# Attention kernel on one core: PE rounds of two steps, scores in four PSUM banks, stacked heads for the out-projection, one 1024-column exponential

## The chip, the cores and the metric

The kernel runs on one core of a Trainium2 chip. The metric is device microseconds of one execution, taken as the median of several runs. The engines are named as in the profile: PE is TensorE (PEld its weight loads), DVE VectorE, ACT ScalarE, POOL GpSimd, SP the engine that here issues nearly all the DMAs. Each engine works through its own queue in order, and they meet at semaphores.

## The reference

Input `x` is 4 x 1024 x 128 in f32. One pre-norm transformer layer is computed:

```
x = x + attention(layernorm(x))         # 16 heads of 64, rotary on the first 32, no mask
x = x + ffn(layernorm(x))               # low rank: x U1 V1 -> gelu -> U2 V2 (rank 32, width 512)

q, k, v = heads(x Wq), heads(x Wk), heads(x Wv);  q, k = rope(q), rope(k)
attn = softmax(q k^T / 8);  out = concat(attn v) Wout + bout
```

Attention is nearly all of it: 64 pairs of batch and head, each with a 1024 x 1024 score matrix.

## The kernel before

Heads are taken in groups of `GH` = 4 (16 iterations: 4 batches x 4 groups). A head has `KT` = 8 blocks of 128 keys, so an iteration has `STEPS` = 32 steps, and there are 512 steps in all. Iteration 0 and iteration 15 are written out, iterations 1 to 14 are a hardware loop.

A step `t` of head `h` and key block `kt` does this:

- **Scores** (`pe_scores`, L386 and L387): keys on the partitions, all 1024 queries as columns, in two halves of 512. Q and K are split into a high and a low f16 part and stacked, so a half takes two accumulating full-array matmuls. The result is `S`, 128 x 1024 f32, two PSUM banks, one copy.
- **Exponential** (`act_step`, L516): ScalarE takes each half of `S` and writes `PF`, which has `SLOTS` = 8 slots of 128 x 1024 f32.
- **Values** (`pe_values`, L398): `PF` of the step `PV_LAG` = 2 back, times V (128 x 64, f32), added up over the head in one PSUM bank `O`: columns tiled in two, one half of the queries in each 64 partitions. `O` has two copies, heads alternate.
- **Unit** (`pe_unit`, L407, and `dve_max`, L603): for the row maximum of the head that comes `LEAD` = 12 steps later, an eighth of the queries (128) against all keys into `M`, 128 x 1024, two banks, one copy: two matmuls on 64 rows each, side by side in the array. VectorE takes the maximum over the 1024 columns. The next unit waits for this (`max_read`). The eight maxima go through ScalarE and a DMA into a row of Q's stack, where they are subtracted inside the score matmul.
- **Sums for the denominators** (`pool_sum`, L676, `dve_sum`, L610 and L613): GpSimd adds two slots of `PF` at each even step, VectorE adds those pairs to `SUM`.
- **Tiles** (`pe_tiles`): at chosen steps PE also does a tile of other work into one of two banks `T`: projections of Q, K and V for the next group (L310, L316), the denominators of two heads (`den_tile`, L326: a matmul with ones), and the out-projection (`out_tiles`, L338: two tiles at one step, 64-row matmuls for the two query halves side by side in the array, summed over two heads). Which step has which tile stands in `QK_AT`, `V_AT`, `DEN_AT` and `OUT_AT`. The tile is then read by ScalarE (`act_tiles`, at the front of ScalarE's step) and by VectorE (`dve_tiles`, one step later): rotary product and shuffle L530 and L532, low part L535, add to X L539. GpSimd finishes the rotation (`rot_add` L652 and L655, `rot_low` L663). PE waits before tile n for the readers of tile n - 2 (`before`, `freed`).

PE's order inside a step is values, tiles, scores, unit (`pe_step`). VectorE's is tile readers, sums, the inverse of the denominators (L619), the norm of two heads' output (`dve_norm`, L625), the maximum. The order of SP's queue is written out in `HAND_ORDER`: the new Q and K are handed from `STAGE` to `QK` by four DMAs a head (`hand_over`, L708 and L709), which can start only when GpSimd's last low part is done (`rot_lo`) and the head's scores have been read, and which the unit of step 20 waits for (`handed`). `max` is the row of maxima, `sums`, `inverse` and `spread` are the denominators' way out to be inverted and back, spread over 64 partitions, into `RB`; `wo` is a load of the output weights for two heads.

Ahead of the loop stand the first projections and 12 units; behind it the last denominators, the out-projection and the feed-forward part.

Of the kernel before, what the change touches and what calls it, by code (L numbers as in the profile page):

```python
# [15 lines left out]
P = 128  # L16
# [12 lines left out]
PV_LAG = 2  # L29
# [20 lines left out]
APPLY_AT = (17, 18, 19, 20, 25, 26)  # L50
BIAS_AT = (19, 21, 23, 24, 27, 28)
TURN_X0_AT = (23, 24, 25, 26, 29, 30)
TURN_X_AT = (4, 6, 9, 11, 14, 16)
DOWN_AT = (7, 12, 13, 15, 18, 19)

HAND_ORDER = [("qk", 3), ("wo", 0), ("max", 1), ("sums", 1), ("inverse", 1), ("spread", 1), ("max", 2), ("qk", 0),
              ("qk", 1), ("wo", 1), ("sums", 0), ("max", 3), ("inverse", 0), ("spread", 0), ("qk", 2), ("max", 4)]


def tiles_of(first, last):  # L60

    out = []
    for t in range(STEPS):
# [12 lines left out]
        if t in OUT_AT and not (first and OUT_AT[t]):  # L76
            out += [(t, "out", (OUT_AT[t], z)) for z in range(2)]
# [6 lines left out]
assert PRE_TILES % 2 == 0 and MID_TILES % 2 == 0  # L84


class Iteration:


    def __init__(self, i, first=False, last=False):  # L90
        self.i, self.first, self.last = i, first, last
        self.tiles = tiles_of(first, last)
        self.tile0 = PRE_TILES if first else PRE_TILES + FIRST_TILES + (i - 1) * MID_TILES
        self.turn = 0 if first else FIRST_TILES % 2
# [11 lines left out]

    def bank(self, n):
        return (n + self.turn) % 2


def build(nc, x_d, wq_d, wkv_d, wout_d, bout_d, u1_d, v1_d, b1_d, u2_d, v2_d, b2_d, rope_d, ident_d, out_d):
    with ExitStack() as ctx:
# [15 lines left out]
        WO = sb("WO", [P, 2, 2, D], F32)  # L128
# [54 lines left out]
        HB = [half[:, z * 512:(z + 1) * 512] for half in (S, M) for z in range(2)]  # L183


        x_in = [sem(f"x_in{b}") for b in range(B)]
        w_in, small_in, rope_in = sem("w_in"), sem("small_in"), sem("rope_in")
        wo_in = [sem(f"wo_in{p}") for p in range(2)]
# [47 lines left out]
        def before(it, n):  # L236

            if n >= 2:
                return it.tiles[n - 2][1:], it
            if it.first:  # L240
                return ("proj", PROJ[-2 + n]), Iteration(-1)
            prev = Iteration(it.i - 1) if not (isinstance(it.i, int) and it.i == 1) else Iteration(0, first=True)
            return prev.tiles[n - 2][1:], prev
# [55 lines left out]
        def proj_tile(e, args, g, bank):  # L299
# [5 lines left out]
            if w == "v":  # L305
                cols = bass.ds((gi * GH + 2 * c) * DH, 2 * DH)
                for r in range(4):
                    rows = bass.ds(b * N + (4 * t + r) * P, P)
                    for n, (xp, wp) in enumerate(((0, 0), (0, 1), (1, 0))):
                        mm = e.matmul(T[bank][:, r * P:(r + 1) * P], XT[:, xp, rows], WV[:, wp, cols],  # L310
# [810 lines left out]
```

## Time and profile before

| | |
|---|---|
| median of 3 runs | 1562.38 us (1561.53 to 1564.28) |
| profiled execution | 1561.73 us, of it the span of the instructions 1559.8 us |
| mean granted PE clock | 0.988 of 2.4 GHz |
| busy: PE, DVE, POOL, ACT | 1481, 1170, 969, 753 us |
| instructions | 26676 |

The busy time of an engine is the time in which at least one of its instructions runs. Matmuls are pipelined and their ends modelled, so what a matmul costs PE is read from the start of one group to the start of the next, not from its duration. A line of the timeline merges equal instructions that follow each other and gives their count as x4; what stands in brackets is the idle time in front, and who ended it.

### The profile page before, as it was taken

To read this page: it belongs to the slowest core of one execution; us is meant where nothing else is said; L and a number is where in the kernel's file an instruction comes from. 1 tells how busy PE (TensorE), PEld (TensorE's weight loads), DVE (VectorE), ACT (ScalarE), POOL (GpSimd) and SP (SyncE) were. 2 spreads that over 40 slices of the span, in tenths; PEclk is the share of its full clock that TensorE was granted. 3 is DMA by queue.
4 is the path that set the end of the run, shared out by engine and by line. 5 is a ranking of instruction groups with operands and counts; after the bars stand their busy time and mean duration, and the time that the engine had idled before them with its cause. 6 is when DMAs were issued, how large, how long until landed. Compare 5 with 4: busy or idle time off the path is not lost.

```text
span 1559.8 us, 26676 instructions
## 1 busy us (share of the span) xinstructions
PE 1481.2 (95%) x7801; PEld 504.4 (32%) x7801; DVE 1169.7 (75%) x1297; ACT 752.9 (48%) x1448; POOL 969.3 (62%) x501
## 2 busy tenths in 40 slices
PE   3799999999999999999999999999999999999887
PEld 1233333333333333333333333333333333333324
DVE  7778777778777777877777777777777787777834
ACT  2254545444454544545454454545444454544464
POOL 4498857657384756748475664847566584757831
PEclk9799999999999999999999999999999999999998
DMA  4322031222203122220313122131312212131002
GB/s 145 75 45 58 15 79 26 61 52 57 58 14 78 36 62 41 57 58 14 78 37 69 32 58 57 24 68 37 78 24 58 57 34 61 34 78 24 19 17 66
DMA packets 78386, 79.69 MB, mean 51 GB/s; under 512 B 28212, under 2 KB 45112, under 8 KB 78104
## 3 DMA queue, kind: packets, MB, share of 16 engines
q1 hardware_dynamic: 76912, 78.36, 22.1%
q10 hardware_dynamic: 1448, 1.00, 0.2%
q8 instruction: 14, 0.23, 0.1%
q14 instruction: 12, 0.10, 0.0%
HBM read 26.23 MB, written 2.36 MB: 18 GB/s over the span
## 4 chain that ended last, share of the span: by engine, by line
PE 73%; DVE 10%; POOL 8%; issue 7%; ACT 1%; DMA 1%; SPq 0%; DVEq 0%; POOLq 0%; ACTq 0%
PE O L398 25%; PE S L386 12%; PE S L387 11%; PE M L407 10%; PE TILE L316 5%; DVE MX L603 5%; POOL SA L676 4%; PE TILE L338 4%; PE TILE L310 3%; PE TILE L326 2%; DVE SUM L613 1%; DVE OS L625 1%; POOL STAGE L663 1%; POOL QK L812 1%; POOL RSTD L277 1%
## 5 line engine op out<-in xcount | busy, mean ns | idle before, releaser
L676 POOL TENSOR_TENSOR SA<-PF 128x1024 f32<-128x1024 f32 x256 | 632.4, 2475 | 378.3 <-DVE SUM L610 194.6
L603 DVE TENSOR_REDUCE MX<-M 128x1 f32<-128x1024 f32 x506 | 617.1, 1220 | 314.5 <-PE M L407 312.5
L516 ACT ACTIVATE PF<-S 128x512 f32<-128x512 f32 x1024 | 555.5, 595 | 479.8 <-PE S L387 479.8
L398 PE MATMUL O<-PF,V 128*64 128x512 f32 x2048 | 552.1, 618 | 0.0
L386 PE MATMUL S<-QK 128*128 128x512 f16 x1024 | 392.4, 383 | 1.6 <-DVE MX L603 1.6
L387 PE MATMUL S<-QK 128*128 128x512 f16 x1024 | 389.1, 380 | 0.0
L407 PE MATMUL M<-QK 64*128 64x512 f16 x1012 | 222.8, 437 | 29.8 <-DVE MX L603 23.2
L613 DVE TENSOR_TENSOR SUM<-SUM,SA 128x1024 f32<-128x1024 f32 x128 | 199.0, 1555 | 7.9 <-POOL SA L676 7.9
L386 PEld LDWEIGHTS S<-QK 128*128 128x128 f16 x1024 | 99.7, 97 | 309.7 <-ACT PF L516 188.3
L652 POOL TENSOR_TENSOR T<-T,ROPE 128x512 f32<-128x512 f32 x60 | 76.5, 1274 | 139.3 <-DVE T L532 139.3
L407 PEld LDWEIGHTS M<-QK 64*128 64x128 f16 x1012 | 72.5, 139 | 247.7 <-issue 204.3
L398 PEld LDWEIGHTS O<-PF,V 128*64 128x64 f32 x2048 | 101.3, 134 | 118.9 <-ACT PF L516 79.1
L387 PEld LDWEIGHTS S<-QK 128*128 128x128 f16 x1024 | 100.6, 98 | 75.9 <-issue 0.8
L316 PE MATMUL TILE<-XT,WQK 128*128 (+1 forms) x384 | 108.6, 394 | 5.5 <-DVE XT L1019 2.5
L655 POOL TENSOR_TENSOR YR<-T 128x512 f32<-128x512 f32 x60 | 101.4, 1690 | 4.7
L663 POOL TENSOR_TENSOR STAGE<-YR,STAGE 128x512 f16<-128x512 f32 x64 | 88.3, 1380 | 17.3 <-ACT STAGE L454 17.3
L610 DVE TENSOR_TENSOR SUM<-SA 128x1024 f32<-128x1024 f32 x64 | 79.6, 1243 | 18.0 <-POOL SA L676 18.0
L436 ACT ACTIVATE STAGE<-TILE 128x512 f16<-128x512 f32 x64 | 38.2, 597 | 94.2 <-PE TILE L316 94.2
L444 ACT ACTIVATE V<-TILE 128x512 f32<-128x512 f32 x64 | 38.2, 597 | 89.2 <-PE TILE L310 89.2
L625 DVE TENSOR_TENSOR OS<-OS,RB 128x1024 f32<-128x1024 f32 x32 | 71.3, 2229 | 9.6 <-DMA RB<-den 9.6
L338 PE MATMUL TILE<-WO,OS 64*128 64x128 f32 x1024 | 67.5, 283 | 8.9 <-DVE OS L625 5.9
L338 PEld LDWEIGHTS TILE<-WO,OS 64*128 64x128 f32 x1024 | 61.3, 192 | 34.4 <-issue 33.6
(75 smaller groups left out, 732.6 us busy)
## 6 DMA issues: line engine op xcount, KB each, us to landing
QK<-STAGE SPq DMA_DIRECT2D x128, 256.0 KB, 3.9
QK<-STAGE SPq DMA_DIRECT2D x128, 128.0 KB, 3.1
RB<-den SPq DMA_DIRECT2D x128, 128.0 KB, 2.9
WO<-in_L_attn_Wout SPq DMA_DIRECT2D x64, 64.0 KB, 2.8
X<-in_L_attn_queries SPq DMA_DIRECT2D x4, 512.0 KB, 12.7
RT<-DS SPq DMA_DIRECT2D x128, 2.0 KB, 1.7
out<-X SPq DMA_DIRECT2D x8, 256.0 KB, 2.4
WRAW<-in_L_attn_Wkv SPq DMA_DIRECT2D x1, 1024.0 KB, 8.6
```

The costliest lines, as they stand in the source:

```text
L316: mm = e.matmul(T[bank][:, :], WQK[:, "qk".index(w), wp, kind, cols], XT[:, xp, rows], start=(n == 0), stop=(n == 2))
L338: mm = e.matmul(T[banks[z]][:, j * P:(j + 1) * P], OS[rows, parity, hh, j * P:(j + 1) * P], WO[rows, parity, hh, :], start=(hh == 0), stop ...
L386: e.matmul(S[:, rows], KHL[:, h, keys], QHH[:, h, rows], start=True, stop=False)
L387: e.matmul(S[:, rows], KMH[:, h, keys], QML[:, h, rows], start=False, stop=True).then_inc(scored, 1)
L398: mm = e.matmul(O[h % 2][DH * z:DH * z + DH, :], V[:, h, kt * DH:(kt + 1) * DH], PF[:, t % SLOTS, z * HALF:(z + 1) * HALF], start=(kt == 0 ...
L407: mm = e.matmul(bank[:, keys], QHH[rows, place, q:N:KT], (KHL, KMH)[c][rows, place, keys], start=True, stop=True)
L516: e.activation(PF[:, t % SLOTS, z * HALF:(z + 1) * HALF], S[:, z * HALF:(z + 1) * HALF], ACT.Exp, scale=EXP_SCALE).then_inc(exped, 1)
L603: e.tensor_reduce(MX[:, place % 2, q:q + 1], bank[:, :], AX, ALU.max).then_inc(max_read, 1)
L613: e.tensor_tensor(SUM[:, h % 2, :], SUM[:, h % 2, :], SA[:, part - 1, :], ALU.add).then_inc(summed, 1)
L655: e.tensor_tensor(YR[:, :], T1[:, :], T2[:, :], ALU.add).then_inc(rot_sum, 1)
L663: e.tensor_tensor(LOW[w][:, 0, cols], YR[:, :], HIGH[w][:, 0, cols], ALU.subtract).then_inc(rot_lo, 1)
L676: e.tensor_tensor(SA[:, (t // 2) % 2, :], PF[:, t % SLOTS, :], PF[:, t % SLOTS + 1, :], ALU.add).then_inc(two_summed, 1)
```

## The change

- PE works in rounds of two steps (`pe_step`): at an even step the values of two steps (4 and 3 back; `PV_LAG` is 4), the unit, the scores, the tiles; at an odd step the scores, the tiles, the unit.
- `S` has two copies (four banks), used by even and odd steps. For these banks `O` has one copy and `T` has one; PE waits before a tile for the readers of the one just before it. In the prologue and the tail, halves of `M` stand in as second banks.
- ScalarE's step has one exponential over 1024 columns, and its tile readers stand behind the exponential instead of in front. `exped` counts steps and not halves.
- The out-projection: two heads are stacked on the 128 partitions of `OS` (ScalarE copies `O` out in two pieces of 64 partitions), so each tile is four 128-row matmuls per 512 queries, and the two tiles (query halves) stand at steps of their own. All of `Wout` lies in SBUF, loaded once at the start; `weights_over` and its DMAs are gone.
- The steps of nearly all tiles, inverses, sums and statistics are moved, as the tables show. VectorE's inverse stands before the sum in a step. SP's spread does not wait for the norm any more.
- The 12 leading units go round three pairs of banks instead of two.

```diff
-PV_LAG = 2
+PV_LAG = 4
-QK_AT = (1, 3, 4, 6, 7, 9, 11, 12)
-V_AT = {8: (1, 0), 10: (1, 1), 21: (0, 0), 22: (0, 1)}
-DEN_AT = {5: 1, 20: 0}
+QK_AT = (1, 3, 5, 7, 9, 11, 13, 15)
+V_AT = {8: (1, 0), 10: (1, 1), 22: (0, 0), 24: (0, 1)}
+DEN_AT = {6: 1, 20: 0}
 INVERT_AT = {9: 1, 23: 0}
 NORM_AT = {16: 1, 26: 0}
-OUT_AT = {17: 1, 28: 0}
-SUM_AT = {6: 0, 1: 1, 3: 2}
-STATS_AT = {6: 2, 22: 3}
+OUT_AT = {17: (1, 0), 19: (1, 1), 28: (0, 0), 30: (0, 1)}
+SUM_AT = {7: 0, 1: 1, 3: 2}
+STATS_AT = {6: 2, 14: 3}
...
-        S = pb("S", [P, N], F32)
+        S = pb("S", [P, 2, N], F32)
         M = pb("M", [P, N], F32)
-        O = [pb(f"O{n}", [P, HALF], F32) for n in range(2)]
-        T = [pb(f"TILE{n}", [P, 512], F32) for n in range(2)]
+        O = pb("O", [P, HALF], F32)
+        T = pb("TILE", [P, 512], F32)
...
-            if n >= 2:
-                return it.tiles[n - 2][1:], it
+            if n >= 1:
+                return it.tiles[n - 1][1:], it
...
-        def out_tiles(e, q, parity, i, banks):
-            e.wait_ge(wo_in[parity], 32 * (i + 1))
+        def out_tile(e, q, parity, pair, z, bank):
             e.wait_ge(normed, q + 1)
             for j in range(4):
-                for hh in range(2):
-                    for z in range(2):
-                        rows = slice(DH * z, DH * z + DH)
-                        mm = e.matmul(T[banks[z]][:, j * P:(j + 1) * P], OS[rows, parity, hh, j * P:(j + 1) * P],
-                                      WO[rows, parity, hh, :], start=(hh == 0), stop=(hh == 1))
+                mm = e.matmul(bank[:, j * P:(j + 1) * P], OS[:, parity, z, j * P:(j + 1) * P], WO[:, pair, :],
+                              start=True, stop=True)
...
-                wait(e, exped, 2 * n + z - 1)
+                wait(e, exped, n - 1)
...
         def pe_step(e, it, t):
-            for back in (t - PV_LAG,):
-                if back >= 0:
-                    pe_values(e, it.step(back), it.i * GH + back // KT, back, it.i)
-                elif not it.first:
-                    pe_values(e, it.step(back), it.i * GH - 1, back + STEPS, it.i - 1)
-            pe_tiles(e, it, t)
-            pe_scores(e, it, t)
-            u = t + LEAD
-            if not (it.last and u >= STEPS):
-                ...
-                pe_unit(e, it.step(u), place, q, M)
+            u = t + LEAD
+            if t % 2 == 0:
+                for back in (t - PV_LAG, t - PV_LAG + 1):
+                    if back >= 0:
+                        pe_values(e, it.step(back), it.i * GH + back // KT, back, it.i)
+                    elif not it.first:
+                        pe_values(e, it.step(back), it.i * GH - 1, back + STEPS, it.i - 1)
+                if not (it.last and u >= STEPS):
+                    pe_next_unit(e, it, u)
+            pe_scores(e, it, t)
+            pe_tiles(e, it, t)
+            if t % 2 == 1 and not (it.last and u >= STEPS):
+                pe_next_unit(e, it, u)
...
-            for z in range(2):
-                e.wait_ge(scored, 2 * n + z + 1)
-                ...
-                e.activation(PF[:, t % SLOTS, z * HALF:(z + 1) * HALF], S[:, z * HALF:(z + 1) * HALF], ACT.Exp,
-                             scale=EXP_SCALE).then_inc(exped, 1)
+            e.wait_ge(scored, 2 * n + 2)
+            ...
+            e.activation(PF[:, t % SLOTS, :], S[:, t % 2, :], ACT.Exp, scale=EXP_SCALE).then_inc(exped, 1)
+            act_tiles(e, it, t)
...
-            e.activation(OS[:, h // 2, h % 2, :], O[h % 2][:, :], ACT.Copy).then_inc(o_copied, 1)
+            for z in range(2):
+                cp = e.activation(OS[rows, h // 2, z, :], O[DH * z:DH * z + DH, :], ACT.Copy)
+            cp.then_inc(o_copied, 1)
...
-                wait(sp, normed, q)
-        def weights_over(sp, it, p):
-        ...
+            sp.dma_start(WO[:, :, :], wout_d.rearrange("(c p) n -> p c n", p=P)).then_inc(wo_in, 16)
```

## Rows read from the trace of the kernel before

**Rows 1.** The page, part 1: busy time of each engine.

```profile
PE 1481.2 (95%) x7801; PEld 504.4 (32%) x7801; DVE 1169.7 (75%) x1297; ACT 752.9 (48%) x1448; POOL 969.3 (62%) x501
```

**Rows 2.** Busy time of each engine in one middle iteration of 32 steps.

```profile
677.28:767.62 90.34, 89.12 (x475) 29.88 (x473) 69.13 (x69) 44.45 (x87) 56.67 (x29) 1.00 0.22 50
```

**Rows 3.** PE's timeline over a step without tile: start, duration, line, tile.

```profile
729.91 1.08 PE L398 MATMUL O<-PF,V 128*64 128x512 f32 x4
730.92 0.39 PE L386 MATMUL S<-QK 128*128 128x512 f16 x1
731.15 0.38 PE L387 MATMUL S<-QK 128*128 128x512 f16 x1
...
731.58 0.38 PE L387 MATMUL S<-QK 128*128 128x512 f16 x1
731.89 0.44 PE L407 MATMUL M<-QK 64*128 64x512 f16 x2
732.26 1.08 PE L398 MATMUL O<-PF,V 128*64 128x512 f32 x4
```

**Rows 4.** The same timeline, a unit that waits.

```profile
737.08 0.44 PE L407 MATMUL M<-QK 64*128 64x512 f16 x2 [0.42 <-DVE MX L603]
```

**Rows 5.** PE's timeline behind the last step, two value groups together.

```profile
1506.64 0.38 PE L387 MATMUL S<-QK 128*128 128x512 f16 x1
1506.94 1.94 PE L398 MATMUL O<-PF,V 128*64 128x512 f32 x8
1508.82 0.60 PE L954 MATMUL S<-STAGE,V1P 96*128 96x512 f16 x2
```

**Rows 6.** PE's timeline near the start of the first iteration.

```profile
58.03 0.65 PE L407 MATMUL M<-QK 64*128 64x512 f16 x2
58.61 1.46 PE L316 MATMUL TILE<-XT,WQK 128*128 128x512 f16 x3
```

**Rows 7.** PE's timeline: an out-projection, and full-array f32 tiles in the tail.

```profile
740.81 2.06 PE L338 MATMUL TILE<-WO,OS 64*128 64x128 f32 x32
...
1547.29 1.06 PE L980 MATMUL TILE<-V,QK 128*128 128x128 f32 x8
```

**Rows 8.** ScalarE's timeline, the exponentials of the step of rows 3.

```profile
731.57 1.09 ACT L516 ACTIVATE PF<-S 128x512 f32<-128x512 f32 x2 [1.09 <-PE S L387]
```

**Rows 9.** VectorE's timeline, two maxima.

```profile
732.38 1.22 DVE L603 TENSOR_REDUCE MX<-M 128x1 f32<-128x1024 f32 x1 [0.44 <-PE M L407]
...
735.81 1.22 DVE L603 TENSOR_REDUCE MX<-M 128x1 f32<-128x1024 f32 x1
```

**Rows 10.** Groups by line, VectorE: count, busy us, mean ns, idle before.

```profile
L613 DVE TENSOR_TENSOR SUM<-SUM,SA 128x1024 f32<-128x1024 f32 x128 | 199.0, 1555 | 7.9 <-POOL SA L676 7.9
L625 DVE TENSOR_TENSOR OS<-OS,RB 128x1024 f32<-128x1024 f32 x32 | 71.3, 2229 | 9.6 <-DMA RB<-den 9.6
L532 DVE STREAM_SHUFFLE T<-TILE 128x512 f32<-128x512 f32 x64 | 46.7, 730 | 0.0
L530 DVE TENSOR_TENSOR T<-TILE,ROPE 128x512 f32<-128x512 f32 x64 | 43.5, 680 | 0.4 <-PE TILE L316 0.4
```

**Rows 11.** GpSimd by line and in the timeline, a hand-over's issue and landing.

```profile
L676 POOL TENSOR_TENSOR SA<-PF 128x1024 f32<-128x1024 f32 x256 | 632.4, 2475 | 378.3 <-DVE SUM L610 194.6 <-ACT PF L516 132.2 <-DVE SUM L613 51.5
L652 POOL TENSOR_TENSOR T<-T,ROPE 128x512 f32<-128x512 f32 x60 | 76.5, 1274 | 139.3 <-DVE T L532 139.3
L655 POOL TENSOR_TENSOR YR<-T 128x512 f32<-128x512 f32 x60 | 101.4, 1690 | 4.7
...
725.74 2.14 POOL L663 TENSOR_TENSOR STAGE<-YR,STAGE 128x512 f16<-128x512 f32 x1
738.27 1.16 POOL L663 TENSOR_TENSOR STAGE<-YR,STAGE 128x512 f16<-128x512 f32 x1
...
741.62 0.68 SPq L709 DMA_DIRECT2D QK<-STAGE  x1
DMA to landing us min/median/max: 3.0/3.9/4.6
```

More of the change, by code:

```diff
@@ L75, in tiles_of @@
             out.append((t, "den", DEN_AT[t]))
-        if t in OUT_AT and not (first and OUT_AT[t]):
-            out += [(t, "out", (OUT_AT[t], z)) for z in range(2)]
+        if t in OUT_AT and not (first and OUT_AT[t][0]):
+            out.append((t, "out", OUT_AT[t]))
     return out
@@ L309, in proj_tile @@
                     for n, (xp, wp) in enumerate(((0, 0), (0, 1), (1, 0))):
-                        mm = e.matmul(T[bank][:, r * P:(r + 1) * P], XT[:, xp, rows], WV[:, wp, cols],
+                        mm = e.matmul(bank[:, r * P:(r + 1) * P], XT[:, xp, rows], WV[:, wp, cols],
                                       start=(n == 0), stop=(n == 2))
@@ L315, in proj_tile @@
                 for n, (xp, wp) in enumerate(((0, 0), (0, 1), (1, 0))):
-                    mm = e.matmul(T[bank][:, :], WQK[:, "qk".index(w), wp, kind, cols], XT[:, xp, rows],
+                    mm = e.matmul(bank, WQK[:, "qk".index(w), wp, kind, cols], XT[:, xp, rows],
                                   start=(n == 0), stop=(n == 2))
@@ L602, in dve_max @@
                 wait(e, max_found, head - 1)
-            e.tensor_reduce(MX[:, place % 2, q:q + 1], bank[:, :], AX, ALU.max).then_inc(max_read, 1)
+            e.tensor_reduce(MX[:, place % 2, q:q + 1], bank, AX, ALU.max).then_inc(max_read, 1)
         def dve_sum(e, head, h, part):
@@ L632, in dve_step @@
                 dve_last(e, t)
-            h, kt = t // KT, t % KT
+            if t in INVERT_AT and not (it.first and INVERT_AT[t]):
+                dve_invert(e, it.pair(INVERT_AT[t]))
             if kt in SUM_AT and SUM_AT[kt] == 0:
@@ L637, in dve_step @@
                 dve_sum(e, it.i * GH + h - 1, (h - 1) % GH, SUM_AT[kt])
-            if t in INVERT_AT and not (it.first and INVERT_AT[t]):
-                dve_invert(e, it.pair(INVERT_AT[t]))
             if t in NORM_AT and not (it.first and NORM_AT[t]):
                 dve_norm(e, it.pair(NORM_AT[t]), NORM_AT[t])
-            u = t + LEAD
             if not (it.last and u >= STEPS):
-                dve_max(e, it.step(u), it.i * GH + u // KT, (u // KT) % GH, u % KT, M)
+                dve_max(e, it.step(u), it.i * GH + u // KT, (u // KT) % GH, u % KT, M[:, :])
         def rot_add(e, args, g):
@@ L672, in pool_sum @@
         def pool_sum(e, t, pair, free):
-            e.wait_ge(exped, 4 * pair + 4)
+            e.wait_ge(exped, 2 * pair + 2)
             wait(e, summed, free)
@@ L729, in den_over @@
                 sp.wait_ge(inverse_turned, 16 * (q + 1))
[L730 removed]
                 for s in range(4):
                     hh, z = s // 2, s % 2
[L733 removed]
+                    sp.dma_start(RB[DH * hh:DH * hh + DH, z, :],
                                  den_d[s:s + 1, :].broadcast_to([DH, HALF])).then_inc(spread_in, 16)
[L736 to L742 removed]
         def sp_iteration(sp, it):
@@ L778, in build @@
         tail0 = lastit.tile0 + len(lastit.tiles)
-        den_bank = lastit.bank(len(lastit.tiles))
         @block.sync
@@ L942, in body @@
                 for t in range(STEPS):
+                    if it.first and OUT_AT.get(t) == (0, 0):
+                        e.wait_ge(wo_in, 16)
                     pe_step(e, it, t)
@@ L998, in _ @@
                 if c == 1:
-                    kind, args = lastit.tiles[-1][1:]
-                    pe.wait_ge(*freed(kind, args, lastit))
                     pe.wait_ge(den_copied, PAIRS)
-                    out_tiles(pe, PAIRS - 1, 1, GROUPS - 1, (1 - den_bank, den_bank))
+                    for z in range(2):
+                        out_tile(pe, PAIRS - 1, 1, HEADS // 2 - 1, z, TB[z])
                 if c == 3:
                     for late in range(EARLY, FC):
-                        down_tile(pe, late, late % 2)
+                        down_tile(pe, late, TB[late % 2])
                 if c >= 1:
```

161 lines of the change are left out of this document (75 added, 86 removed).

## The prediction

> **What bounds the kernel now.** I read the page's first part, then the busy time of whole loop iterations, then TensorE's timeline inside one of them, and last VectorE's rows. PE is busy for 95% of the span, VectorE for 75%, GpSimd 62%, ScalarE 48% [rows 1]. A middle iteration of 32 steps takes 90.34 us with PE busy for 89.12 [rows 2]; sixteen of these are 1445 of the 1559.8 us of the span. The feed-forward part begins behind the last step at 1508.82 [rows 5]. In the timeline PE runs without a hole: a step without a projection tile goes from one value group (729.91) to the next (732.26), so 2.35 us [rows 3]. The reader is to see the seams in it: the values take 1.01 us to the first score, scores 0.97 to the unit M, the unit 0.37 to the next values. Scores are full-array, units are two row tiles of 64, values two column tiles of 64. Two scores further PE is 0.43 us further (731.15 to 731.58), so one is 0.215 and four with a seam make 0.97: the seam from scores to M is 0.11 us; the unit's 512 columns would be 0.21 too, so its seam is 0.16. The kernel is thus bound by the order of PE's queue, not by ScalarE: S being free late shows only as early weight loads that wait under a running value group. Real PE holes are few: M waits for the previous maximum, as at 737.08 with 0.42 us [rows 4], and about as much once more near the other out-projection: 1.2 us an iteration, the 90.34 less the 89.12 of busy time.
>
> **The change, part by part.**
>
> *The order of PE's queue.* Two steps now cost 4.70 us. In the new order a pair is: values of two steps, M, scores, scores, M (tiles stand behind each score block). Two value groups together are shown behind the last step: eight matmuls start at 1506.94 and the next operation at 1508.82, 1.88 us, where two separate groups take 2.02 [rows 5]. Two score blocks that touch take 0.97 + 4 x 0.215 = 1.83 us, where two separate ones take 1.94. M to values stays 0.37. Values to M is not in the trace; I take it like values to scores, with no change, and bound it by a gain or a loss of 0.05 (the span of the seams seen). M straight to full-array work stands only at the start, at the lower clock: M at 58.03, tile at 58.61, 0.58 us [rows 6], of which 0.43 are columns at 1.2 GHz, so a seam of 0.15. At 2.4 GHz it lies between the 0.10 of scores to M and the 0.16 of M to values; I take 0.13, so 0.34 us. The pair: 1.88 + 0.34 + 1.83 + 0.37 = 4.42, which saves 0.28 us. 512 steps are 256 pairs: 72 us, with bounds of 51 and 92 (0.08 either way for both seams together).
>
> The Trainium skill says in TensorEngine Tiling (Array Packing), Key Properties, that changing the tiling mode drains TensorE, while changing only the tile does not. The rows agree as to where the seams are: at each of the three changes of [rows 3]. By that rule alone, at one equal price of 0.16 for each change, six changes a pair become four, and 256 pairs would give back 82 us; the rows price them unequally, so my 72 stands.
>
> *Tiles.* The projections are the same instructions, now beside scores of the same form: no change. The denominator tile stood between values and scores and stands now between two score blocks; it gets one more seam of 0.09 (scores to values, 1506.64 to 1506.94, less 0.215) [rows 5]: 32 x 0.09 = 3 us lost. The out-projection had 32 half-row matmul records in 2.06 us for both tiles; it becomes two tiles of 8 full records. The same form (128 rows, 128 columns, f32) stands in the tail, 8 records in 1.06 us [rows 7]. So stacking heads halves the count and gains nothing: 2 x 1.06 against 2.06, some 2 us lost over 32 pairs; bounded by 5 us either way, as its seams to the scores vanish. Together -5 us.
>
> *One exponential of 1024 columns.* Two of 512 take 1.08 us with their overlap [rows 8]; one of 1024 has the same columns, so between 1.0 and 1.1, and I take 1.04. ScalarE is not on the path, S has two copies, and values come four steps late, so all this is worth nothing by itself. What hides it is two steps of PE work (4.4 us). The copies out are two of 64 partitions and not one of 128, 0.6 us more per head, with the same cover.
>
> *One tile bank in place of two.* Each tile on PE now waits until the previous one has been read, and ScalarE reads it behind the exponential. It matters where tiles stand in an even and the next odd step and ScalarE reads the first: steps 8 and 9, 10 and 11 (V, then a projection), and 6 and 7. Before, the first half's exponential at 731.57 starts 0.42 after that half's second score at 731.15 [rows 3, 8]. The one of step 8 then starts 3 x 0.215 + 0.42 = 1.07 us after that step's first score, ends after 1.04, the copy of V (512 columns) takes 0.60, and PE gets the bank at 2.75. PE is there at 0.86 + 0.65 + 0.86 = 2.37, a little later with the seams of V's twelve matmuls. So a hole of 0.35 us twice, none behind the denominators: 0.7 us an iteration. Everywhere else 0.37 + 1.88 + 0.34 + 0.86 = 3.45 us lie between two tiles, more than the 3.0 in which VectorE is through with a maximum, a product and a shuffle.
>
> *M against VectorE.* M has one copy. The maximum starts 0.49 after M (731.89, then 732.38), lasts 1.23 [rows 9], and a waiting M starts 0.05 after it (735.81 + 1.23, then 737.08); the next VectorE instruction can start after 1.15. So M to M is never under 1.77. The new PE spacings are 0.34 + 1.83 = 2.17 plus tiles from the even M to the odd, and 0.37 + 1.88 = 2.25 from the odd to the next even: both longer, without VectorE's other work. I carried that work through 32 steps, each maximum starting at the later of "its M + 0.49" and "the previous maximum + 1.15 + the other work", with the mean durations: sums 1.55 (steps 1, 3 and, at the most, 7 of each head), product and shuffle 1.4 at steps 2, 6, 10, 14, norm 2.2 at 16 and 26 [rows 10]. VectorE works some 69 us of 88, so it catches up mostly. It is late at two places: at 16 the norm puts M of 17 off by 0.2 and with the sum of 17 that of 18 by 0.45; at 26 the norm puts 27 off by 0.65 and 28 by 0.45. That is 1.75 us an iteration, against 1.2 before.
>
> The Trainium skill (GPSIMD Engine Reference, Specifications) says that GpSimd shares SBUF interfaces with VectorE and contends with its instructions of two SBUF inputs. The sum's mean of 1.55 us against 1.23 for the maximum, which reads one input over the same columns, agrees. By that rule shorter iterations overlap these more; that way is rival B below, whose price comes from rows.
>
> *Hand-over of Q and K.* The last rotated tile moves from step 11 to 13, so GpSimd's last low part moves from step 15 to 17, while M of step 20 still needs the first head's hand-over. In the trace, low part ended at 739.43, its fourth transfer was issued at 741.62 and lands 3.9 later: 6.1 us [rows 11]. By the spacings above, product and shuffle of step 14 end 40.1 us into the new iteration; GpSimd then does 3.0 of rotation and two sums of 2.48 until 48.0, and the low part of 1.2 until 49.2; handed over at 55.3. M of 20 is due at 56. The cover is under 1 us; I put 0.3 us an iteration on it. SP's queue in front is shorter (two weight transfers and the wait on the norm left it). The denominators' way has 2.5 to 3 steps to the inverse; if that is 1 us short, VectorE waits and not PE, inside its slack of 19 us.
>
> *The rest.* Output weights are loaded once in the prologue (512 KB behind X, needed at step 28): nothing. The 12 leading units use three banks, but VectorE's 1.15 a maximum sets their pace: nothing. In the tail four value groups stand there and not two, the other two left the loop. The first iteration has VectorE's statistics at steps 6 and 14 beside a product and shuffle; I take 2 us more stall for it and 2 for the last.
>
> *Sum.* New holes an iteration 0.7 + 1.75 + 0.3 = 2.75, old 1.2, so 1.55 x 15 = 23 us, and 4 for the ends: 27. -72 + 5 + 27 = -40 us. The profiled execution took 1561.7 us (span 1559.8); minus 40 is 1521.7, and the median of the runs is 0.7 above it: 1522 us.
>
> **Rivals.**
> A: the holes do not come (tile reads are sooner, VectorE's late moments fall into slack). For it: 20 us an iteration of VectorE are free. Against: the norm's 2.2 us plus two maxima and a sum (6.1) are longer than a pair (4.4). Time: 1562 - 72 + 5 + 4 = 1499.
> B: VectorE becomes the bound in stretches. A low part of GpSimd takes 2.14 us at one place and 1.16 at another [rows 11]; if VectorE's eight sums of steps 1 and 3 and its two norms were each 1 us longer in the same way, a pair, which leaves 4.42 - 2.3 - 1.55 = 0.57 us beside two maxima and a sum, would hide 0.57 of each. Of the other 0.43, 4.3 us an iteration, I estimate that a third finds no tile to hide behind: 1.4 x 15 = 22 us. Time: 1544. Against: GpSimd's work is the same, and the means hold both kinds.
> C: slower. The hand-over becomes the end of the chain. Step 20's M waits at the head of PE's queue, with scores, tiles and all values behind it, and VectorE and ScalarE soon wait for these. If each of the five GpSimd instructions in front is 1 us longer (as 2.14 is than 1.16) [rows 11], it is handed over at 60.3: a hole of 4.3 us, 4.0 beyond the forecast, in each of 15 iterations, 60 us: 1582. It makes the kernel slower once the hole passes 2.7 us (40 / 15) beyond what I have in. Against: the low part at just this place took 1.16.
> D: the change does not do what it says, because a seam is paid at each group of matmuls whatever stands next. Then the 72 us go and so do most holes, for PE is as slow as before: 1562. Against: the 1.88 us of [rows 5].
>
> **How the numbers follow.** The forecast 0.52, A 0.14, B 0.17, C 0.12, D 0.05. The time is the forecast's, 1522. The range reaches to A's 1499 and past B towards no change, which takes in most of the seams' bounds: 1499 to 1558. Of this kernel 0.2%, 3 us, is what can be told from no change. Faster: forecast, A, B, less a little: 0.81. Same 0.06, slower 0.13.
>
> **What would show it.** Right: PE's timeline has eight value matmuls in 1.88 us, M to scores 0.34, a plain pair of 4.4 us, and an iteration of 87.7 us; waits of M for the maximum near steps 17, 18, 27, 28; a tile at steps 9 and 11 that waits for ScalarE's copy of V by 0.35 us; next to no wait of M for the hand-over. Wrong: plain pairs of 4.6 us or more (the seams), more than 4 us of holes per iteration (VectorE or tile bank), or a wait of M for the hand-over of over 1 us in each iteration.

## The result, and the profile after

The changed kernel takes 1568.10 us (median; 1566.81 to 1569.64) against 1562.38 (1561.19 to 1564.28): a ratio of 1.0034, 95% interval 1.0022 to 1.0046, so a little slower. The forecast was 1522 us and a range that ended at 1558; both were wrong. Rows of before are named by their groups in the section of rows.

The page of the changed kernel, part 1 and the first line of part 4, against [rows 1], and below it the first line of part 4 of the kernel before:

```profile
PE 1429.6 (91%) x7289; PEld 548.1 (35%) x7289; DVE 1225.1 (78%) x1297; ACT 746.3 (48%) x1000; POOL 972.5 (62%) x501
...
PE 38%; issue 18%; POOL 17%; DVE 15%; DMA 5%; ACT 4%; SPq 2%; DVEq 0%; POOLq 0%; ACTq 0%
```

```profile
PE 73%; DVE 10%; POOL 8%; issue 7%; ACT 1%; DMA 1%; SPq 0%; DVEq 0%; POOLq 0%; ACTq 0%
```

PE is busy for 51.6 us less, as meant, and the span is still 5.2 us longer (1565.0). VectorE does the same 1297 instructions in 55 us more. In the chain that ended last, PE had 73% before and has 38% now; the rest went mostly to issue, POOL and VectorE.

Busy time of each engine in a middle iteration of the changed kernel, against [rows 2] (window, length, PE, PEld, DVE, ACT, POOL, clock):

```profile
682.47:772.70 90.23, 85.67 (x442) 32.63 (x441) 72.90 (x69) 43.93 (x58) 56.82 (x28) 1.00 0.21 47
```

An iteration is as long as before (90.34) with 3.45 us less PE work in it. The clock is full in both. So the loop lost nothing and gained nothing: what the seams gave was spent on holes. PE's timeline in this iteration shows both (start, duration; in brackets the idle time in front and what ended it):

```profile
700.99 0.44 PE L397 MATMUL M<-QK 64*128 64x512 f16 x2 [0.66 <-DVE MX L600]
...
737.65 0.44 PE L397 MATMUL M<-QK 64*128 64x512 f16 x2
738.02 1.94 PE L388 MATMUL O<-PF,V 128*64 128x512 f32 x8
739.89 0.44 PE L397 MATMUL M<-QK 64*128 64x512 f16 x2
740.26 0.39 PE L376 MATMUL S<-QK 128*128 128x512 f16 x1
...
742.78 1.15 PE L330 MATMUL TILE<-WO,OS 128*128 x8 [0.62 <-DVE OS L622]
...
746.95 0.43 PE L397 MATMUL M<-QK 64*128 64x512 f16 x2 [0.78 <-DVE MX L600]
747.32 0.39 PE L376 MATMUL S<-QK 128*128 128x512 f16 x1
...
750.04 0.44 PE L397 MATMUL M<-QK 64*128 64x512 f16 x2
...
752.86 0.44 PE L397 MATMUL M<-QK 64*128 64x512 f16 x2 [0.52 <-DMA QK<-STAGE]
...
766.77 1.94 PE L388 MATMUL O<-PF,V 128*64 128x512 f32 x8
768.64 0.44 PE L397 MATMUL M<-QK 64*128 64x512 f16 x2
...
770.53 0.38 PE L377 MATMUL S<-QK 128*128 128x512 f16 x1
772.33 0.44 PE L397 MATMUL M<-QK 64*128 64x512 f16 x2 [1.42 <-DVE MX L600]
772.70 1.51 PE L388 MATMUL O<-PF,V 128*64 128x512 f32 x6
```

M to values takes 0.37 (737.65 to 738.02), eight value matmuls 1.87 and M to scores 0.37 (739.89 to 740.26, where 0.34 was forecast): the seams are nearly there as forecast. The pair from 766.77 to 772.70 takes 5.93, of which the last M's wait is 1.49 (by the distance to the score in front of it), so 4.44 without it. Earlier in the same iteration, the two tiles of steps 9 and 11 wait for ScalarE:

```profile
718.62 0.83 PE L306 MATMUL TILE<-WV,XT 128*128 x12
720.56 0.82 PE L312 MATMUL TILE<-XT,WQK 128*128 x3 [0.24 <-ACT V L441]
```

By distances between starts, the holes of one iteration are: 0.73 where M of step 2 waits for a maximum (at 700.99), 0.42 and 0.41 at the tiles of steps 9 and 11, 0.9 at the out-projection of 17 (it waits for the norm), 0.85 at M of 18, 0.58 at M of 20 (the hand-over), 1.49 at M of 27; with 0.15 at M of step 0 that is 5.5 us. The kernel before has 1.35 by the same count (0.86 and 0.49). The busy times make it 4.6 and 1.2 only, since the modelled ends of the records in front reach a little into each hole.

The groups by line (busy us, mean ns, idle before) that answer to [rows 10, 11]:

```profile
L673 POOL TENSOR_TENSOR SA<-PF 128x1024 f32<-128x1024 f32 x256 | 614.9, 2416 | 377.6 <-DVE SUM L607 265.6 <-DVE SUM L610 57.8 <-ACT PF L513 54.2
...
L600 DVE TENSOR_REDUCE MX<-M 128x1 f32<-128x1024 f32 x504 | 614.4, 1219 | 233.0 <-PE M L397 232.9
L610 DVE TENSOR_TENSOR SUM<-SUM,SA 128x1024 f32<-128x1024 f32 x128 | 247.2, 1931 | 4.1 <-POOL SA L673 4.0
...
L622 DVE TENSOR_TENSOR OS<-OS,RB 128x1024 f32<-128x1024 f32 x32 | 83.4, 2607 | 6.2 <-DMA RB<-den 6.2
```

The maximum is as long as ever. The sum went from 1555 ns to 1931, the norm from 2229 to 2607, with shapes unchanged. Why shows in the two timelines side by side, first GpSimd's, then VectorE's, around the wait of M at 772.33:

```profile
761.43 4.67 POOL L673 TENSOR_TENSOR SA<-PF 128x1024 f32<-128x1024 f32 x2 [8.59 <-DVE SUM L607]
767.70 2.36 POOL L673 TENSOR_TENSOR SA<-PF 128x1024 f32<-128x1024 f32 x1 [1.60 <-ACT PF L513]
773.55 2.35 POOL L673 TENSOR_TENSOR SA<-PF 128x1024 f32<-128x1024 f32 x1 [3.49 <-DVE SUM L610]
```

```profile
765.15 2.04 DVE L610 TENSOR_TENSOR SUM<-SUM,SA 128x1024 f32<-128x1024 f32 x1
767.11 1.21 DVE L600 TENSOR_REDUCE MX<-M 128x1 f32<-128x1024 f32 x1
768.24 2.90 DVE L622 TENSOR_TENSOR OS<-OS,RB 128x1024 f32<-128x1024 f32 x1
771.06 1.21 DVE L600 TENSOR_REDUCE MX<-M 128x1 f32<-128x1024 f32 x1
772.20 1.21 DVE L610 TENSOR_TENSOR SUM<-SUM,SA 128x1024 f32<-128x1024 f32 x1
```

GpSimd's pair ends at 766.10, and VectorE's sum 1.09 later (767.19). GpSimd's next ends at 770.06, VectorE's norm 1.08 later (771.14). The sum at 772.20, with GpSimd idle, takes 1.21. The maximum at 767.11 takes 1.21 too, though GpSimd runs from 767.70: it has one input, and that in PSUM. So a VectorE instruction with two SBUF inputs that meets a running GpSimd instruction stands until that has ended and then takes some 1.1 us. The maximum behind the norm could have begun at 769.4 and began at 771.06, and M, with all of PE behind it, waited for it.

The whole trace bears this out. Of VectorE's 224 sums and norms, 172 start while a GpSimd instruction runs; 171 of these end 1.05 to 1.20 us after its end, and so take 1.21 to 3.38 us, by how much of it was left. None of the other 52 takes more than 1.23. Of the maxima, 260 start under a GpSimd instruction with over 0.3 us left, and none takes more than 1.23. If the two engines shared the time between them, the ends would not lie at one distance. In the kernel before, 114 of the 224 meet a running GpSimd instruction. What these take beyond 1.22 us each adds up to 77 us before and to 140 after.

The Trainium skill has this rule, in "SBUF — State Buffer", "SBUF: two separate sides": of a VectorE instruction with two SBUF inputs and a GpSimd instruction that reads SBUF, whichever starts first has the shared pair of ports for its whole instruction and the other fully blocks. The trace agrees, with the 2.90 us above where the free length is 1.2.

The same could be read from the kernel before. Its larger hole is at M of step 27, behind a norm that took 2.74 us and ended (678.92) 1.08 after GpSimd's pair sum (677.84). The first line is PE's, the second VectorE's, the third GpSimd's:

```profile
680.12 0.44 PE L407 MATMUL M<-QK 64*128 64x512 f16 x2 [0.79 <-DVE MX L603]
```

```profile
676.18 2.74 DVE L625 TENSOR_TENSOR OS<-OS,RB 128x1024 f32<-128x1024 f32 x1
```

```profile
675.49 2.35 POOL L676 TENSOR_TENSOR SA<-PF 128x1024 f32<-128x1024 f32 x1 [2.45 <-ACT PF L516]
```

The middle iterations, from the first score of step 32 to that of step 480, take 1264.7 us before and 1263.5 after (90.33 and 90.25 each). The lead and the first iteration are 3.1 us longer, the last is 0.3 shorter, and from the last step's first score to the end it is 57.3 against 53.9. These sum to the 5.2.

### The profile page after: what moved, and what is told of

It is laid out like the page before. It is cut to its first block, busy times and chain, and to the rows that moved or that the text cites. A ratio compares the mean times of both kernels' runs of the same rounds, so it can differ in the third digit from the quotient of the medians.

```text
span 1565.0 us, 23905 instructions
## 1 busy us (share of the span) xinstructions
PE 1429.6 (91%) x7289; PEld 548.1 (35%) x7289; DVE 1225.1 (78%) x1297; ACT 746.3 (48%) x1000; POOL 972.5 (62%) x501
## 4 chain that ended last, share of the span: by engine, by line
PE 38%; issue 18%; POOL 17%; DVE 15%; DMA 5%; ACT 4%; SPq 2%; DVEq 0%; POOLq 0%; ACTq 0%
PE O L388 11%; POOL SA L673 10%; PE S L376 7%; PE S L377 6%; PE M L397 6%; DVE MX L600 5%; DVE SUM L610 5%; DMA QK<-STAGE 4%; POOL STAGE L660 3%; PE TILE L312 3%; PE TILE L322 2%; ACT PF L513 2%; PE TILE L330 1%; SPq L705 1%; POOL T L649 1%
## 5 line engine op out<-in xcount | busy, mean ns | idle before, releaser
L673 POOL TENSOR_TENSOR SA<-PF 128x1024 f32<-128x1024 f32 x256 | 614.9, 2416 | 377.6 <-DVE SUM L607 265.6
L513 ACT ACTIVATE PF<-S 128x1024 f32<-128x1024 f32 x512 | 515.3, 1022 | 632.4 <-PE S L377 589.7
L388 PE MATMUL O<-PF,V 128*64 128x512 f32 x2048 | 496.9, 606 | 0.0
L397 PE MATMUL M<-QK 64*128 64x512 f16 x1008 | 222.0, 437 | 70.8 <-DVE MX L600 52.8
L610 DVE TENSOR_TENSOR SUM<-SUM,SA 128x1024 f32<-128x1024 f32 x128 | 247.2, 1931 | 4.1 <-POOL SA L673 4.0
L388 PEld LDWEIGHTS O<-PF,V 128*64 128x64 f32 x2048 | 124.5, 136 | 206.6 <-issue 187.5
L494 ACT ACTIVATE OS<-O 64x512 f32<-64x512 f32 x128 | 75.7, 591 | 116.9 <-PE O L388 116.1
L622 DVE TENSOR_TENSOR OS<-OS,RB 128x1024 f32<-128x1024 f32 x32 | 83.4, 2607 | 6.2 <-DMA RB<-den 6.2
L330 PE MATMUL TILE<-WO,OS 128*128 (+1 forms) x504 | 69.0, 280 | 16.1 <-DVE OS L622 13.7
L330 PEld LDWEIGHTS TILE<-WO,OS 128*128 128x128 f32 x504 | 65.6, 194 | 30.8 <-issue 20.8
L536 DVE TENSOR_TENSOR X<-TILE,X 128x512 f32 (+1 forms) x63 | 43.2, 686 | 29.4 <-PE TILE L330 29.4
```

The lines of the kernel that those rows point to most:

```text
L330: mm = e.matmul(bank[:, j * P:(j + 1) * P], OS[:, parity, z, j * P:(j + 1) * P], WO[:, pair, :], start=True, stop=True)
L388: mm = e.matmul(O[DH * z:DH * z + DH, :], V[:, h, kt * DH:(kt + 1) * DH], PF[:, t % SLOTS, z * HALF:(z + 1) * HALF], start=(kt == 0), stop ...
L397: mm = e.matmul(bank[:, keys], QHH[rows, place, q:N:KT], (KHL, KMH)[c][rows, place, keys], start=True, stop=True)
L513: e.activation(PF[:, t % SLOTS, :], S[:, t % 2, :], ACT.Exp, scale=EXP_SCALE).then_inc(exped, 1)
L610: e.tensor_tensor(SUM[:, h % 2, :], SUM[:, h % 2, :], SA[:, part - 1, :], ALU.add).then_inc(summed, 1)
L673: e.tensor_tensor(SA[:, (t // 2) % 2, :], PF[:, t % SLOTS, :], PF[:, t % SLOTS + 1, :], ALU.add).then_inc(two_summed, 1)
```

## Experiments

Each is the changed kernel with the edit shown, unless it says otherwise. Ratios are to the kernel before, with their 95% interval. "An iteration" is the mean over the fourteen middle ones.

**Without most of GpSimd's pair sum.** The sum runs over 32 columns in place of 1024, so most of the denominators' sums is left out. `SA` is filled with ones once at the start, and VectorE still adds all its columns.

```diff
-            e.tensor_tensor(SA[:, (t // 2) % 2, :], PF[:, t % SLOTS, :], PF[:, t % SLOTS + 1, :],
+            e.tensor_tensor(SA[:, (t // 2) % 2, 0:32], PF[:, t % SLOTS, 0:32], PF[:, t % SLOTS + 1, 0:32],
```

> The changed kernel with GpSimd's sum over 32 columns in place of 1024 (it leaves out most of the denominators' sums; VectorE's sums keep all columns). Theory L (VectorE is late at M because its two-input sums and norms stand still until GpSimd's running sum has ended): VectorE's L610 sum falls from a mean of 1.93 to 1.25 us, the norm from 2.61 to about 1.3, the holes before M of steps 2, 8-9, 18, 27 go; an iteration falls from 90.2 to about 87 us, the kernel to about 1515. Theory T (single tile bank and ScalarE's order): holes of 0.42 twice stay, iteration 89.5 or more. Theory H (hand-over) also gains: M of 20 waits no longer, 0.5 us of the iteration.

Measured: 1490.73 us, 0.9538 (0.9523 to 0.9552); an iteration takes 85.67 us. By line, VectorE:

```profile
L610 DVE TENSOR_TENSOR SUM<-SUM,SA 128x1024 f32<-128x1024 f32 x128 | 161.5, 1262 | 0.6 <-POOL SA L673 0.4
...
L622 DVE TENSOR_TENSOR OS<-OS,RB 128x1024 f32<-128x1024 f32 x32 | 38.9, 1215 | 9.9 <-DMA RB<-den 9.9
```

Its unchanged sum and norm are 1.26 and 1.22 us, and of the middle iteration's holes only the two at the tiles and the small one at M of step 0 are left. 77 us go, 24 more than expected. PE's waits in the whole trace fell from 52.8 to 8.8 us for the maximum, from 13.7 to 6.4 for the norm, and from 16.9 to 7.9 for the hand-over (6.5 of these stand ahead of the loop in both kernels).

**The same edit on the kernel before** (it leaves out the same).

> The kernel before with GpSimd's sum over 32 columns in place of 1024 (it leaves out most of the denominators' sums). Theory L says that the old order had slack for VectorE's long sums and norms: only its 1.2 us of holes an iteration can go and some of the first and last iteration and of the tail, so 1530 to 1545, an iteration of 89.1 us, where the changed kernel fell by 77 us. If GpSimd's sum costs both kernels alike (a stall on PE or ScalarE that has nothing to do with M), it falls by 70 to 80 us: 1485 to 1495.

Measured: 1535.81 us, 0.9829 (0.9813 to 0.9845); 27 us go. The busy time in 720 us of its middle:

```profile
680.00:1400.00 720.00, 720.00 (x3812) 241.10 (x3812) 536.96 (x559) 359.02 (x697) 164.10 (x227) 1.00 0.23 51
```

PE has no idle time at all in 720 us. The same GpSimd work costs the old order 27 us and the new one 77. And between the two kernels without it lie 45 us (1535.8 to 1490.7): an iteration takes 88.97 in the one and 85.67 in the other, which is 4.3 us less of PE's work and 1.0 more of holes. The change does what it says once GpSimd keeps out of VectorE's way. That 45 is near the forecast's 40 is partly luck, since the forecast had 1.55 us more of holes an iteration and 4 more at the ends.

**The pair sum in two pieces of 512 columns.** If the standing instruction is released when GpSimd's instruction ends, shorter ones release it sooner; if the two merely slow each other, nothing changes.

```diff
-            e.tensor_tensor(SA[:, (t // 2) % 2, :], PF[:, t % SLOTS, :], PF[:, t % SLOTS + 1, :],
-                            ALU.add).then_inc(two_summed, 1)
+            for z in range(2):
+                half = slice(z * HALF, (z + 1) * HALF)
+                ts = e.tensor_tensor(SA[:, (t // 2) % 2, half], PF[:, t % SLOTS, half],
+                                     PF[:, t % SLOTS + 1, half], ALU.add)
+            ts.then_inc(two_summed, 1)
```

> The changed kernel with GpSimd's sum of 1024 columns as two instructions of 512. Theory L1 (VectorE's two-input SBUF instruction stands still until the GpSimd instruction that runs at that moment has ended, and then takes its own 1.2 us): GpSimd's work stays about 2.4 us a sum, but the longest stand-still is halved from 2.4 to 1.2 us; L610's mean falls from 1.93 to some 1.6, the norm's from 2.61 to under 2.1, the kernel by 10 to 30 us, to 1540 to 1558. Theory L2 (both share bandwidth by the element while they overlap): splitting changes nothing, means stay, 1565 to 1575.

Measured: 1547.96 us, 0.9908 (0.9893 to 0.9924); an iteration 88.72 us. By line:

```profile
L675 POOL TENSOR_TENSOR SA<-PF 128x512 f32<-128x512 f32 x512 | 725.7, 1447 | 318.7 <-DVE SUM L607 267.3 <-ACT PF L513 28.9 <-DVE SUM L610 22.5
...
L610 DVE TENSOR_TENSOR SUM<-SUM,SA 128x1024 f32<-128x1024 f32 x128 | 220.8, 1725 | 6.6 <-POOL SA L675 4.7
...
L622 DVE TENSOR_TENSOR OS<-OS,RB 128x1024 f32<-128x1024 f32 x32 | 49.1, 1534 | 7.6 <-DMA RB<-den 7.6
```

GpSimd works more (726 us against 615) and the kernel is 20 us faster: what hurts is how long one GpSimd instruction holds on. The norm fell from 2607 ns to 1534. The price of GpSimd's extra time shows in PE's waits (us in total, times, longest):

```profile
PE M L397 <- DMA QK<-STAGE: 35.4, 16, 6.5
PE M L397 <- DVE MX L600: 20.0, 27, 2.8
```

```profile
PE M L397 <- DVE MX L600: 52.8, 57, 2.8
PE M L397 <- DMA QK<-STAGE: 16.9, 16, 6.5
```

The first block is this kernel, the second the changed one. The waits for the maximum shrank by 33 us, and those for the hand-over grew by 18.5. In this trace too the sums and norms end at one distance from the end of the GpSimd instruction that they met (186 of 187 within 1.05 to 1.20 us), and none takes more than 2.33 us, where it was 3.38.

**The same split on the kernel before.**

> The kernel before with GpSimd's sum as two instructions of 512. L1 and the slack of the old order: at the most what the small sum gave, 26 us; the holes of 0.42 and 0.79 shrink, 5 to 12 us, 1550 to 1558. L2: no change, 1562.

Measured: 1552.17 us, 0.9934 (0.992 to 0.9948): 10 us, half of what it is worth in the new order. Sum and norm went to 1444 and 1751 ns.

**The norm of head 1 earlier.**

```diff
-NORM_AT = {16: 1, 26: 0}
+NORM_AT = {13: 1, 26: 0}
```

> The changed kernel with the norm of the odd pair at step 13 in place of 16. Theory L: the holes of 0.9 (tile of 17 waits for the norm) and of part of 0.85 (M of 18) go, some 1.3 us of an iteration, 20 us in all: 1548. If the norm's place doesn't matter (VectorE bound by its total): 1567.

Measured: 1561.03 us, 0.9989 (0.9979 to 0.9998); an iteration 89.68. It gives 7 us, with the sum's mean at 2021 ns and the norm's at 2462: it moves the standing instruction to a place with more slack and does not shorten it by much. 20 us had been expected. The hole at the tile of step 17 went, but M of 18 waits longer (1.08 us of idle time in place of 0.77).

**The first sum of a head one step earlier.**

```diff
-SUM_AT = {7: 0, 1: 1, 3: 2}
+SUM_AT = {6: 0, 1: 1, 3: 2}
```

> The changed kernel with the first VectorE sum of each head at its step 6, as before, in place of 7. GpSimd's third and fourth sums of a head can then start a step earlier and stand closer to their data. Tail: the last denominators' tile comes about 3 us earlier (it was 3.8 us later than in the kernel before, counted from the last scores). Inside the loop theory L says the sum now stands in an even step with product and shuffle, so M of 7 is later by up to 0.8 in each head with such a tile, but GpSimd's backlog at steps 0 to 3 is gone: between -1 and +1 us an iteration. In all 1550 to 1575; the tail's 3 us are the firm part.

Measured: 1576.80 us, 1.0088 (1.0075 to 1.0101), 9 us slower. VectorE's sums by line, and PE's first wait:

```profile
L610 DVE TENSOR_TENSOR SUM<-SUM,SA 128x1024 f32<-128x1024 f32 x128 | 183.6, 1434 | 4.6 <-POOL SA L673 4.5
```

```profile
PE M L397 <- DVE MX L600: 71.3, 59, 2.8
```

The sums stand less (1434 ns against 1931), VectorE is busy 53 us less, and the wait at M of step 2 is gone. Yet M waits 71 us in all and not 53, for M of step 7 has a new wait. First VectorE's line, then PE's:

```profile
720.38 1.30 DVE L607 TENSOR_TENSOR SUM<-SA 128x1024 f32<-128x1024 f32 x1 [2.47 <-ACT DS L471]
```

```profile
722.88 0.44 PE L397 MATMUL M<-QK 64*128 64x512 f16 x2 [1.65 <-DVE MX L600]
```

This is not GpSimd's hold but an ordinary wait. In the code the first sum of a head waits until ScalarE has copied the denominators out (`den_copied`), since their tile reads the `SUM` that it overwrites. The change moved that tile from step 5 to 6, so a sum at step 6 stands at the head of VectorE's queue, with VectorE idle for 2.47 us and the maximum behind it. 1.65 us more there and 0.7 less at M of 2 are about the 0.9 us by which an iteration is longer (91.12). From the last step's first score to the end this kernel takes 56.0 us, so the sum's place explains 1.3 of the tail's 3.5 us, where 3 were expected.

**Tiles read ahead of the exponential.** ScalarE's turn is changed, so that it empties the single tile bank first.

```diff
+            act_tiles(e, it, t)
             e.wait_ge(scored, 2 * n + 2)
             ...
             e.activation(PF[:, t % SLOTS, :], S[:, t % 2, :], ACT.Exp, scale=EXP_SCALE).then_inc(exped, 1)
-            act_tiles(e, it, t)
```

> The changed kernel with ScalarE's tile readers in front of the exponential of their step, as before. Theory T: the two holes of 0.42 us in front of the tiles of steps 9 and 11 go, 0.85 x 14 = 12 us: 1556. Theory L: they go, but PE is only earlier at the next wait for VectorE, so half of it stays: 1562.

Measured: 1549.71 us, 0.9918 (0.9905 to 0.9931); an iteration 88.95. The holes of steps 9 and 11 are gone. It is worth 1.3 us an iteration, more than their 0.83 and more than expected (1556 at best). The rest is mostly at M of 27, whose wait fell from 1.42 to 0.79 us of idle time, with the norm's mean down to 1931 ns. That this comes from ScalarE's instructions standing at other times is not shown.

**Both of these together** (tiles first, norm at 13).

> The changed kernel with ScalarE's tile readers in front of the exponential and the odd pair's norm at step 13. If the two gains are separate: 0.9918 x 0.9954 of the changed kernel's ratio, 1549.7 - 7 = 1543 us, an iteration of 88.4 us. If the one only moves PE into the other's wait: 1548 or more.

Measured: 1546.64 us, 0.9903 (0.9887 to 0.992). Of the 7 us that the norm's move gave alone, 3 are left: M of 18 now waits 1.17, where it waited 0.77 with the tiles first alone.

**Two exponentials of 512 columns.**

```diff
-            e.activation(PF[:, t % SLOTS, :], S[:, t % 2, :], ACT.Exp, scale=EXP_SCALE).then_inc(exped, 1)
+            for z in range(2):
+                ex = e.activation(PF[:, t % SLOTS, z * HALF:(z + 1) * HALF],
+                                  S[:, t % 2, z * HALF:(z + 1) * HALF], ACT.Exp, scale=EXP_SCALE)
+            ex.then_inc(exped, 1)
```

> The changed kernel with two exponentials of 512 columns in a step in place of one of 1024. My theory: ScalarE is off the path, only the tile readers behind it come 0.06 us later (1.08 against 1.02), twice an iteration: 1568 to 1570. If ScalarE's order is more on the path than thought: over 1575.

Measured: 1571.46 us, 1.0057 (1.004 to 1.0074), 3 us slower than the changed kernel, which is hardly clear of the noise, as the two intervals overlap. An iteration is 0.23 us longer (90.48): 0.14 of it at the tiles of steps 9 and 11, which are read later, and 0.08 at M of 27. So the single exponential is not where the time went.

**Steps one by one on PE,** with the rest of the change kept: values, tiles, scores and M per step as before. ScalarE copies `O` out one step later for it (a line not shown here).

```diff
-            if t % 2 == 0:
-                for back in (t - PV_LAG, t - PV_LAG + 1):
-                    ...
+            for back in (t - PV_LAG,):
+                ...
+            pe_tiles(e, it, t)
             pe_scores(e, it, t)
-            pe_tiles(e, it, t)
-            if t % 2 == 1 and not (it.last and u >= STEPS):
+            if not (it.last and u >= STEPS):
                 pe_next_unit(e, it, u)
```

> The changed kernel with PE's order of one step: values of t - 4, tiles, scores, M (the copy out one step later for it); four banks for the scores, single tile bank, stacked heads and one exponential stay. If the seams are worth what PE's busy time shows, the plain pair is 4.70 in place of 4.44 us and the M waits shrink, as M to M is 2.35 and more: an iteration of 90 to 92 us, time 1565 to 1590. If rounds of two cause the M holes and give nothing else, it is faster than the changed kernel: under 1562.

Measured: 1726.61 us, 1.1051 (1.1033 to 1.107), an iteration 100.1. A plain step takes 2.35 us again, so the seams come back, but that is only part of it. PE's timeline:

```profile
699.96 1.11 PE L306 MATMUL TILE<-WV,XT 128*128 x12 [1.64 <-DVE T L526]
```

With one tile bank, tiles of neighbouring steps stand until VectorE or ScalarE has read the last one; in rounds, values and scores of two steps lie between most of them. By idle time these stands are 6.6 us an iteration, against 0.5 in rounds. So this run doesn't price the rounds alone, as it was meant to (1565 to 1590 was expected). It shows that with the tiles at these steps the single bank is cheap only in rounds.

**Split, tiles first, norm at 13.**

> Split sum, ScalarE's tile readers first, odd norm at step 13. L1: 10 us or more below 1546.6, so 1525 to 1537, an iteration of 87.6 us or less. L2: 1545 to 1550.

Measured: 1531.31 us, 0.9801 (0.9788 to 0.9815); 87.64 an iteration.

**Split, tiles first, norm at 14, last Q and K tiles earlier.** The split made GpSimd's hand-over late, so its last tiles move forward.

```diff
-QK_AT = (1, 3, 5, 7, 9, 11, 13, 15)
+QK_AT = (1, 3, 5, 7, 9, 11, 12, 14)
-NORM_AT = {16: 1, 26: 0}
+NORM_AT = {14: 1, 26: 0}
```

> As the one before, but the last two projections at steps 12 and 14 in place of 13 and 15, the odd norm at 14 in place of 13. The wait of M of step 20 for the hand-over (0.5 us an iteration in the changed kernel) goes, 7 us; the norm in an even step may cost as much at M of 15 or 16. 1520 to 1545.

Measured: 1517.98 us, 0.9714 (0.9701 to 0.9728): 44 us faster than the kernel before and 50 than the changed one. An iteration takes 86.63. Its waits of PE:

```profile
PE M L397 <- DVE MX L600: 35.2, 42, 3.1
```

The hand-over's wait in the loop is gone, only the one of 6.5 us ahead of it is left, and two waits for the maximum remain in an iteration (0.84 at M of 27 and 0.56 at M of 16).

## Why the prediction was wrong, point by point

**Seams: right.** 4.42 us a pair were forecast and 4.44 measured; M to full-array work is 0.37, not 0.34. Rival D falls.

**Tiles: a little better than forecast.** An out tile adds 0.89 us (2.72 from the first score of step 18 to M of step 19, less 1.83 for eight scores), not 1.06. All of PE's work together gave 4.3 us an iteration (5.5 of holes less 1.35, and 0.1 shorter), where I had 4.2.

**One exponential: right** in that ScalarE is not on the path; what little two exponentials cost comes mostly by way of the tile bank.

**One tile bank: right, and a little short.** 0.7 us an iteration forecast, 0.83 measured, at the two places named.

**M against VectorE: the step that failed.** I had 1.75 us an iteration. The wait at M of step 2, those at the out-projection of 17, M of 18 and M of 27 make 0.73 + 0.9 + 0.85 + 1.49 = 4.0. Of the places named, M of 18 and of 27 are right; M of 28 does not wait, at 17 it is the tile that waits for the norm and not M for the maximum, and M of 2 was not named. The step took the mean durations of before, 1.55 and 2.2, as if they were properties of the instructions. They were properties of the overlap with GpSimd: alone these instructions take 1.26 and 1.22, held they reach 3.4. M of 2 waits because a sum took 3.01 us (from 696.80) behind GpSimd's pair sums, M of 27 because a norm took 2.90. In the new order 172 sums and norms meet GpSimd, where 114 did.

The sign that I had in front of me was [rows 10]: a norm over the 1024 columns of the maximum took 2.23 us. I called this a small contention and let it in as rival B, as a uniform microsecond with a third of it uncovered, 22 us. B named the right mechanism with a price that was too small: 1544 against 1568. A second sign was the old hole of 0.79 us at M of 27, behind a norm of 2.74 us, which the prediction's text puts at about the 0.42 of the other.

What shows the cause is the pair of runs without GpSimd's sums, 77 us in the new order against 27 in the old, and the split, 20 against 10. The 50 us between 77 and 27 are about the whole of the miss (46). PE's waits by name part them roughly: with GpSimd's sums left out, the waits for maximum and norm fall by 51 us in the new order and by 20 in the old one (23.2 to 2.9, the norm's even), those for the hand-over by 9 and by nothing. So some 31 of the 50 are held instructions and 9 the hand-over; the rest is not taken apart.

**Hand-over: short.** 0.3 forecast, 0.58 measured. Rival C's 4.3 us hole did not come in the loop, but the split shows how near it is: 0.4 us more of GpSimd per pair sum (726 less 615, over 256) made it 1.80. In the first iteration it did come once, with 2.91 us.

**The ends: wrong.** I had 4 us for stalls in the first and last iteration together and nothing in the tail. The lead and first iteration cost 3.1 net of what the seams gave there, and the tail 3.5. In the first iteration PE is idle for 10.2 us, against 3.8 before. Its largest hole is at M of step 20:

```profile
115.61 0.44 PE L397 MATMUL M<-QK 64*128 64x512 f16 x2 [2.91 <-DMA QK<-STAGE]
```

The change moved one of VectorE's statistics from step 22 to 14, and GpSimd's instruction on it (2.62 us, from 105.89) now stands just in front of the last low part, on which the hand-over waits. Nearly all the other holes of the first iteration are waits for the maximum. In the tail, the last denominator's first sum stands behind the out-projection's addition at 1507.90:

```profile
1507.90 0.69 DVE L536 TENSOR_TENSOR X<-TILE,X 128x512 f32<-128x512 f32 x1 [3.90 <-PE TILE L330]
1508.51 1.22 DVE L607 TENSOR_TENSOR SUM<-SA 128x1024 f32<-128x1024 f32 x1
1512.26 4.68 DVE L610 TENSOR_TENSOR SUM<-SUM,SA 128x1024 f32<-128x1024 f32 x2 [2.54 <-POOL SA L673]
```

GpSimd's last two pair sums wait for it (they start at 1509.87, and the data of the first of them had long been there), and PE's last denominator tile for them: it starts at 1517.09, with 3.80 us of waiting, where before it started at 1511.54. Moving the sum gives 1.3 of the 3.5 back. The rest of the tail was not taken apart.

**In sum.** The middle iterations came out 2.6 us over the forecast's 87.7; over 14 that is 36 of the 45 us by which the span missed, and the ends are the other 9. The chance of 0.13 for slower was placed on a single mechanism (C); the one that struck was in the text with its effect bounded too low. A, with no holes, had 1499; only the run without GpSimd's sums came below that (1491), and it leaves work out.

## What to carry to other kernels

An instruction whose mean is far above that of another over the same columns may be held and not long, as the sums and norms were here: find by what, and carry its free and its held length, not its mean, into a new schedule. Before tightening the order of the engine that bounds, check that the engine which releases it has no two-SBUF-input instruction in front of the release while GpSimd runs; cut GpSimd's long instructions in two (20 us here), or move the held one to a place with slack (7 us here), and measure the order again after each. Before an instruction is moved, look up what it waits for in the code: a wait at the head of VectorE's queue costs as much as a hold (9 us here). Removing 4.3 us of one engine's work from a loop was worth nothing here, because the single-buffered result that it waits for (M) came no sooner.

## What the runs showed that was not expected

- The hold goes both ways. In the changed kernel GpSimd's low part takes 1.16 us free. The one below began at 744.64 while VectorE's sum ran until 745.76 (it had itself stood until the pair sums' end at 744.67), and took 2.13, its end 1.01 behind VectorE's:

```profile
739.03 5.64 POOL L673 TENSOR_TENSOR SA<-PF 128x1024 f32<-128x1024 f32 x2
744.64 2.13 POOL L660 TENSOR_TENSOR STAGE<-YR,STAGE 128x512 f16<-128x512 f32 x1
```

```profile
743.52 2.24 DVE L610 TENSOR_TENSOR SUM<-SUM,SA 128x1024 f32<-128x1024 f32 x1
```

- More GpSimd time can be less kernel time: 726 us of pair sums in halves beat 615 us in wholes by 20 us.
- Less held time can be a slower kernel: with sums at 1434 ns in place of 1931 it took 9 us more, because one of them waited for the denominators' copy in front of a maximum.
